# Store stage folded into the second FFN stage of a software pipeline, with new call orders on four engines

## What is computed

```python
y = einsum('ncij,vc->nvij', patches, w_mask) / (x_norm * w_norm)   # match with 512 prototypes
idx = argmax(y.reshape(NL, -1)); max_ch, max_col = idx // 9, idx % 9
integrate = max_act * max_sim + w_mask[max_ch] * (1.0 - max_sim)
h = leaky_relu(concat([integrate, sim_map_max]) @ w_i1.T + b_i1, 0.2)
vcs = tanh(h @ w_i2.T + b_i2)
h2 = relu(vcs @ w_l1.T + b_l1) @ w_l2.T + b_l2
x = x + fold(einsum('ncij,oc->noij', h2, w_conv))
# per token, q_mul rounds to fp8 e5m2, q_acc to fp16
t = t + q_acc(q_acc(q_mul(relu(qlinear(ln(t), W1, b1))) @ q_mul(W2).T) + q_mul(b2))
```

## Time and profile before

| what | value |
|---|---|
| median of 3 runs | 1993.93 us (1993.76 to 1994.25) |
| the profiled execution | 1996.22 us |
| its span, first to last instruction | 1994.4 us |
| busy: PE, DVE, ACT, POOL | 95%, 94%, 83%, 81% |
| POOL busy in all | 1621.8 us |
| mean granted TensorE clock | 0.985 of full speed |

### The profile page before, as it was taken

One profiled execution on the slowest core, in us unless ns is written; L12 is line 12 of the kernel. 1 busy time (PEld: TensorE's weight loads), 2 busy tenths in 40 slices (PEclk: granted clock), 3 DMA queues, 4 the chain that ended last, 5 costly groups with the idle time before them and its releaser, 6 DMA issues.

```text
span 1994.4 us, 44820 instructions
## 1 busy us (share of the span) xinstructions
PE 1898.1 (95%) x13105; PEld 1429.9 (72%) x13105; DVE 1866.6 (94%) x6525; ACT 1656.4 (83%) x3205; POOL 1621.8 (81%) x1170
## 2 busy tenths in 40 slices
PE   5899999999999999999999999999999999999964
PEld 3567777777777777777777777777777777777642
DVE  7999999999999999999999999999999999999740
ACT  1168888888888888888888888888888888888885
POOL 2578888888888888888888888888888888888752
PEclk9999999999999999999999999999999999999985
DMA  3324545454454545445454454544545455454322
GB/s 96 100 73 129 135 125 147 117 147 125 134 139 117 150 122 139 133 127 145 116 147 126 129 143 117 146 126 133 139 119 151 118 143 129 122 150 118 92 74 71
DMA packets 83890, 249.78 MB, mean 125 GB/s; under 512 B 15736, under 2 KB 17986, under 8 KB 83650
## 3 DMA queue, kind: packets, MB, share of 16 engines
q1 hardware_dynamic: 52866, 170.80, 27.3%
q0 software_dynamic: 28672, 75.52, 18.0%
q10 hardware_dynamic: 2112, 0.60, 0.2%
HBM read 133.23 MB, written 57.02 MB: 95 GB/s over the span
## 4 chain that ended last, share of the span: by engine, by line
PE 72%; DVE 10%; issue 6%; ACT 5%; POOL 3%; DMA 2%; POOLq 0%; SPq 0%; ACTq 0%; DVEq 0%
PE y_ps L648 11%; PE y_ps L650 11%; PE y_ps L649 11%; PE bank L673 9%; PE bank L703 8%; PE bank L685 6%; PE bank L739 4%; ACT y L475 4%; PE bank L754 3%; PE bank L713 3%; DVE best_y L1025 3%; PE bank L723 2%; POOL prod L390 2%; DMA wsel<-proto_rows,w_index 1%; PE bank L711 1%
## 5 line engine op out<-in xcount | busy, mean ns | idle before, releaser
L475 ACT CAST y<-bank 128x384 f16<-128x384 f32 x1152 | 554.1, 481 | 185.9 <-PE bank L673 175.4
L1025 DVE TENSOR_REDUCE best_y<-y_ps 128x2 f32<-128x1024 f32 (+1 forms) x640 | 704.6, 1102 | 0.6 <-PE y_ps L650 0.6
L648 PE MATMUL y_ps<-proto_hi,xh 96*128 96x512 f32 x1152 | 574.1, 498 | 22.5 <-DVE best_y L1025 15.1
L483 ACT ACTIVATE h<-y,f_b 128x1152 f16<-128x1152 f16 x384 | 471.7, 1270 | 0.0
L649 PE MATMUL y_ps<-proto_lo,xh 96*128 96x512 f32 x1152 | 456.5, 396 | 0.0
L650 PE MATMUL y_ps<-proto_hi,xl 96*128 96x512 f32 x1152 | 455.9, 396 | 0.0
L673 PE MATMUL bank<-tqt,f_w 96*128 96x384 f16 x1152 | 390.2, 339 | 42.4 <-ACT y L475 34.7
L411 POOL TENSOR_TENSOR xl<-xc,xh 96x1152 fp32r<-96x1152 f32 x128 | 341.2, 2666 | 26.4 <-ACT xh L538 15.5
L343 POOL DMA_INDIRECT xsel<-x_pm,x_index x128 | 121.6, 950 | 230.0 <-DVE xn L983 216.4
L673 PEld LDWEIGHTS bank<-tqt,f_w 96*128 96x128 f16 x1152 | 110.9, 96 | 262.9 <-issue 144.4
L648 PEld LDWEIGHTS y_ps<-proto_hi,xh 96*128 96x128 f32 x1152 | 221.7, 192 | 84.1 <-issue 39.7
(11 more groups left out here) (131 smaller groups left out, 3874.7 us busy)
## 6 DMA issues: line engine op xcount, KB each, us to landing
xc<-x_cm SPq DMA_DIRECT2D x128, 432.0 KB
xp<-x_pm SPq DMA_DIRECT2D x128, 432.0 KB, 5.4
h<-h POOLq DMA_DIRECT2D x128, 432.0 KB, 4.5
out<-o_pm SPq DMA_DIRECT2D x128, 432.0 KB
xsel<-x_pm,x_index POOLq DMA_INDIRECT x128, 3.7
wsel<-proto_rows,w_index POOLq DMA_INDIRECT x128
proto_rows<-proto SPq DMA_DIRECT2D x1, 384.0 KB, 2.7
proto<-w_mask SPq DMA_DIRECT2D x1, 192.0 KB, 3.3
```

The costliest lines, as they stand in the source:

```text
L475: act.copy(y16[:, q, r * TOK:(r + 1) * TOK], bank[0][:, 0:TOK]).then_inc(s_y16, 1)
L483: act.activation(h16[:, q, :], y16[:, q, :], ACT.Relu, bias=f1_b[:, q:q + 1]).then_inc(s_h16, 1)
L648: pe.matmul(y, hi, proto_hi[:], start=True, stop=False)
L1025: dve.tensor_reduce(best_y[t % 2][:, j0:j1], y_ps[n % 2][:, 0:j1 - j0, :], AX_X, ALU.max).then_inc(s_yd, 1)
```

## The change

Three things are changed, all in the order of calls; no instruction is added or taken away and no shape changes.

- STORE becomes stage 11, the same as FFN2. `ffn2_bias`, `output` and the store of a tile now run in the slot of its `ffn2`, and there are 139 slots in place of 140.
- The slot tables of POOL, ACT, PE and DVE are written in a new order. SP keeps its order.
- On POOL `product` comes before `t_center`, `gather_x` moves from the head to the middle of the slot, and `output` is the last call. On ACT the whole layer 2 copy and `squares` move up between `ffn1_out` 5 and 6. On PE the two `ffn2` calls stand together behind `pick`, and the two `turn` calls stand apart.

```diff
-LOAD, SPLIT, MATCH, SELECT, PICK, MIX, INPUT, HIDDEN, CONV, NORM, FFN, FFN2, STORE = range(13)
+LOAD, SPLIT, MATCH, SELECT, PICK, MIX, INPUT, HIDDEN, CONV, NORM, FFN, FFN2, STORE = 0, 1, 2, 3, 4, 5, 6, 7, 8, 9, 10, 11, 11
...
             def slot(s):
-                gather_x(s)
                 hidden8(s)
                 lock(s)
                 t_norm(s)
+                product(s)
                 t_center(s)
```

More of the change, by code:

```diff
@@ L438, in slot @@
                 t_norm(s)
+                product(s)
                 t_center(s)
-                product(s)
+                low_h(s)
+                gather_x(s)
                 low_x(s)
+                gather_w(s)
                 output(s)
-                low_h(s)
-                gather_w(s)
             run.slots(slot)
@@ L758, in slot @@
             def slot(s):
+                hidden2(s)
+                ffn1(s, 0)
                 match(s, 0)
                 match(s, 1)
-                ffn1(s, 0)
-                hidden2(s)
-                conv(s, 0)
                 match(s, 2)
                 ffn1(s, 1)
-                turn_x(s)
-                match(s, 3)
+                conv(s, 0)
                 ffn1(s, 2)
@@ L1080, in slot @@
                 low_part(s)
-                mix_sims(s)
                 x_dif(s)
@@ L1084, in slot @@
                 x_sq(s)
+                x_norm(s)
                 cos(s)
-                x_norm(s)
+                variances(s)
+                mix_sims(s)
                 mix_row(s)
-                variances(s)
+                root(s, 0)
                 best_j(s)
-                root(s, 0)
+                root(s, 1)
                 one_hot(s)
-                root(s, 1)
-                index(s)
-                normed_x(s)
                 root(s, 2)
@@ L1098, in slot @@
                 root(s, 4)
-                residual(s, 0)
-                root(s, 5)
-                pick_root(s)
-                ffn2_bias(s)
-                root(s, 6)
-                y_max(s, 0)
+                pick_root(s)
+                root(s, 5)
+                index(s)
+                root(s, 6)
+                normed_x(s)
+                residual(s, 0)
                 residual(s, 1)
                 t_mean(s)
+                y_max(s, 0)
+                y_max(s, 1)
+                sims(s)
+                best_v(s)
                 remainder(s)
-                y_max(s, 1)
+                v_index(s)
+                ffn2_bias(s)
+                y_max(s, 2)
                 x_stats(s, [0, 1, 2])
                 x_stats(s, [3, 4])
-                y_max(s, 2)
                 x_stats(s, [5])
+                y_max(s, 3)
                 x_stats(s, [6, 7, 8])
-                sims(s)
-                best_v(s)
-                y_max(s, 3)
-                v_index(s)
                 y_max(s, 4)
```

54 lines of the change are left out of this document (28 added, 26 removed).

## The result

The changed kernel takes 2443.25 us (median of 4 runs, 2442.53 to 2446.55), the kernel before 1994.09 (4 runs beside it). The ratio is 1.225, with a 95% interval from 1.2228 to 1.2271. The prediction was 2013, range 1990 to 2055: the sign was right and the size was not, by a factor of over twenty (449 us in place of 19).

A forecast was written before the change was run, and what follows sets the result against it. The prediction took the longest loop between engines as the slot: 14.76 us (PE and ACT) against 14.60, +0.16 over 120 slots, +19 us, with filling and emptying at 0. Forecast 2013 us, range 1990 to 2055.

The forecast's parts named there:

- first loop: Roots, product and sims across DVE and POOL: 14.56 us a slot, 14.75 with dependent pairs added, bounds 14.56 and 14.96.
- the stretch: DVE's own work from root(s, 6) to sims in the new order, put at 3.72 us.
- POOL's chain: From root(s, 6) on DVE over t_norm and product on POOL to the start of sims, 4.08 us.
- a loop that I haven't seen: Sign that the forecast is wrong: PE waiting elsewhere, at a match for y_max for instance; no size given.
- late cast: POOL's hidden8 cast lands too late behind SP's transfers; landing above 6.5 us decides, at 7.2 time is 2054; chance 0.17.
- The loop of the earlier trace: DVE's root(s, 6) over POOL's t_norm and product to the start of sims, predicted at 4.08 us.
- Dependent neighbours: Four DVE pairs where the second needs the first's result lose 0.19 us a slot together, bounds 0 and 0.4.
- faster: Rival: t_norm, product and hand-overs take 3.7 us, DVE never waits, slot 14.39, time 1969; chance 0.10.
- nothing changes: Rival: dependent pairs cost nothing and PE's rows hide waits; both loops fall to 14.6, time 1994; chance 0.13.
- second loop: PE and ACT: high stands between ffn1_out 3 and 4 while PE waits for the bank; 14.76 us a slot.
- The fold at 0 us: 140 slots become 139, but the slot removed held only the last tile's bias, sum and store; priced at 0 us.
- Filling and emptying: Start and end of the pipeline: same chains in another order, 0 with 5 us either way.

The follow-up runs named there:

- e6: Changed kernel with PE repeating the product of ffn1(s, 7) thirteen more times before it signals; 2452.06 us, ratio 1.2287.
- e2: Changed kernel with only ffn2_bias moved on DVE, from behind v_index to behind the last statistics, ahead of y_max 4; 2119.49 us, ratio 1.0607.
- e10: Changed kernel, all orders kept, with one wait more: POOL's low_x starts only when the slot's bias has ended; 2127.63 us, ratio 1.0671.
- e4: Kernel before with only ffn2_bias moved on DVE, from behind pick_root to behind the last statistics; 2287.43 us, ratio 1.1459.
- e11: e9 with x_dif also made an operation of one input, which leaves out one half of it; 2073.0 us, ratio 1.0400.
- e12: e11 with remainder moved behind v_index on DVE; 2075.0 us, ratio 1.0391.
- e8: e2 with SP's loads spread over the slot, so the cast isn't in flight together with them; 2107.4 us, ratio 1.0574.
- e9: e7 and e8 together: low_part with one input and SP's loads spread, on e2; 2086.9 us, ratio 1.0459.
- e7: e2 with low_part made an operation of one input, its subtraction left out; 2105.8 us, ratio 1.0552.
- e3: Changed kernel's call orders with STORE put back to stage 12, as in the kernel before; 2790.32 us, ratio 1.3982.
- e1: Changed kernel with the bias tile f2_b held in float32 instead of float16; 2506.6 us, ratio 1.2557.

## Why the prediction was wrong, and where it was right

**The step that failed** is the first loop's balance, and the sentence under it: "DVE's work outside the stretch plus POOL's chain". It carried every instruction of DVE with the duration that it had in its old place. The change moved `ffn2_bias` from beside POOL's DMA issues to beside `low_x`, and there its 0.52 us of DVE's time becomes up to 3.7. In place of the 14.56 stands the loop over the held bias, 18.13 us by its rows in e6; with the bias moved away the slot is 15.39 (e2), with `low_x` made to wait for it 15.47 (e10). I had compared the orders of each engine by itself, looking for waits on semaphores, and never laid the new DVE row beside the new POOL row. The text ahead of the prediction says that the engines meet only at semaphores and that nothing else sets the order; e2, e4 and e10 show a second meeting place of DVE and POOL, which no wait in a profile lists. A sign of it could be had from the kernel before: in the slot of the earlier trace rows its bias and its small operations with two inputs (L921, L928, L935 and on) all ran while POOL issued DMAs or stood. The prediction's own list of signs did name what the profile shows, PE waiting at a `match` for `y_max`, as "a loop that I haven't seen".

**The sign** was right, and mostly by luck: 324 of the 449 us come from a mechanism that the prediction doesn't contain. What it does contain is slower too, by 79 us in e11, where the two largest holds and the late cast are gone, against the 19 forecast.

**The loop of the earlier trace rows** was right to 0.02 us: 4.08 predicted, 4.06 in e2, and `sims` waits there for `product` in nearly every slot (26.3 us in 101 times between 200 and 1800 us). In the changed kernel itself it only shows at times (12.8 us in 50 times between 200 and 2200 us), because the longer loop over the bias lies above it.

**Dependent neighbours** were under-sized. The prediction gave the pair `best_v`, `v_index` 0.05; it is 0.16. The row (0.22 apart) already held that; halving it for "one short step between them" was the error. Against the rule of the Trainium skill that I had weighed there (VectorE: DVE Perf Modes, "The DRAIN you can't avoid": a semaphore after each operation costs nothing), e12 shows 0.23 us for one directly dependent pair. The other three pairs weren't measured apart.

**The late cast**, rival with 0.17, is real in e2: the landing went to 6.8 us median there, above the 6.5 that it needed, with ACT waiting for it. In the changed kernel, with its longer slot, it is 6.2 and costs nothing to speak of (1.2 us in 2 waits of ACT). It was worth 12 us by e8 against e2 and 19 by e9 against e7, less than the 41 of the rival, and it added to the forecast instead of taking its place. The rival *faster* fell with the first loop's 4.06, and *nothing changes* with e11 and e12, which are slower by 4% with the holds all but gone.

**The second loop** (`high` inside the hand-over of `bank0`, 14.76) was never the longest in any run, so nothing shows whether its size was right. The stated bounds of the two loops, 2003 to 2032, don't come out of its sums either: 120 slots at the first loop's own upper bound of 14.96 give 43 us more, 2037.

**The fold at 0 us** is not shown either way, since e3 ran into the buffer. The last sum does start 7.0 us before the end, and the wait for `xp` of the earlier trace rows is gone from the changed kernel, both as predicted.

**Filling and emptying**, 0 with 5 us either way, were wrong: 15.5 us together, and about the same in e11 (3.1 and 11.9), where the bias isn't held. POOL of the changed kernel at the end:

```profile
2426.16 1.81 POOL L402 TENSOR_TENSOR o_pm<-t_pm,zb 128x864 f32<-128x864 f32 x1 [7.44 <-DVE zb L991]
2430.30 0.56 POOL L359 DMA_DIRECT2D h<-h  x1 [2.33 <-ACT h L483]
```

`output` now waits there for the bias of its own slot with the next cast queued behind it, and in the kernel before the cast came first. That this is what costs the 9 us is argued from the order and wasn't tested.

**The sum as it came out**, of one usual slot: 14.76 predicted; 18.15 measured. The held bias is 2.76 of the 3.39 between them (18.15 to 15.39, e2). The hold of `low_part` and the late cast together are 0.20 (e9), `x_dif`'s 0.13 (e11). Of the last 0.30, 0.14 is the length that the hold adds to `x_sum` and 0.11 what the pair `best_v`, `v_index` takes beyond its 0.05, both charged in full to the slot, which no run tests; 0.05 stays without a name.

## What to carry to other kernels

When a change moves instructions, lay VectorE's and GpSimd's new rows side by side, and wherever a VectorE instruction with two inputs in SBUF starts under a GpSimd instruction that reads SBUF, charge it the rest of that one and of all that follow it without a gap (3.75 and 5.34 us in e4); where it comes first, charge GpSimd (0.5 us in e4). Such an instruction belongs beside GpSimd's DMA issues or idle time (0.59 us in e2 and e10), or with one input in PSUM (`residual` above), or GpSimd should wait for it when it is off the critical path (e10: one wait more, 316 us less). A duration from a trace is valid for the place where it was measured; a busy total that grows with an unchanged count of instructions is the first sign in a profile that a place has changed.

## What the hardware showed that I hadn't expected

- The hold is larger than the overlap of the rows. A bias that starts 0.69 us before the listed start of `low_x`, and by its 0.59 would be done ahead of it, stands for 3.81 us. With `low_x` made to wait (e10) the same start costs nothing, and neither does it in the changed kernel's own emptying pipeline, where a bias that starts 0.35 into the gather's issue at 2312.09, with no `low_x` behind it, takes 0.59. A ready GpSimd instruction thus seems to take its turn while the gather ahead of it is still being issued, or its listed start comes late; the rows can't tell these two apart.
- The end of a held instruction is 0.47 to 0.48 us behind the end of the holder, whatever its start: a bias that started 0.82 us after `low_x` took 2.35. Of its free 0.59 us, 0.47 are always left when the holder ends, so nearly none of its work gets done while it is held; with the float32 operand of e1 it is 0.92 of 1.04. In e4 the same price falls on POOL when the bias comes first: `low_x` takes 3.14 in place of 2.67.
- PE stands 1.6 to 2.4 us in each slot of the changed kernel. Its granted clock fell from the 2.4 GHz level to the 1.2 GHz level in 42 stretches of 3.4 or 6.8 us among the 77 slots between 300 and 1700 us, from 1003.77 to 1010.60 for instance, 1.9 us after PE had resumed; the mean was 0.94 over 400 us. The kernel before has no such stretch there, and e6, with 13 products more on PE ahead of the wait, has a single one there, and the same usual slot.
